# Attention and mixture-of-experts layer in float32: the two heads' outputs scaled ahead of one 128-row output projection, VectorE's order at the end of the last pair, and a rearranged beginning

## The reference, cut to what matters

```
t     = tokens * rsqrt(mean(tokens^2) + eps) * rms_w
gates = sigmoid(t @ w_gates)                          # one number per token and head
q, k, v = t @ wq[h], t @ wk[h], t @ wv[h]
attn  = softmax(causal(q @ k.T * scale))
out   = (attn @ v) * gates
pred  = sum over heads of out[h] @ wo[h]
x     = layernorm(tokens + pred)
```

## Time and profile before

| | us |
|---|---|
| median of 3 runs | 685.77 |
| lowest and highest | 682.54 and 686.07 |
| the profiled execution, its own time | 684.56 |
| its span (first to last instruction) | 682.8 |

### The profile page before, as it was taken

How to read it: one execution, slowest core, us unless ns; L and a number is a source line. 1 busy time by engine, 2 the same in 40 slices (tenths; PEclk the granted TensorE clock), 3 DMA queues, 4 the chain that set the end, 5 groups by cost and what they waited for, 6 DMA issues and landing times.

```text
span 682.8 us, 15047 instructions
## 1 busy us (share of the span) xinstructions
PE 632.5 (93%) x5338; PEld 513.3 (75%) x5338; DVE 476.1 (70%) x1556; ACT 407.7 (60%) x881; POOL 124.5 (18%) x245
## 2 busy tenths in 40 slices
PE   5999999999999999999999999999984959898975
PEld 2788888778888877888887788888852628888862
DVE  4987777788777778887677888767782525666634
ACT  5866556686655668766566876655651213665643
POOL 6100000020000000000000000000136531776650
PEclk9999999999999999999999999999997989999998
DMA  6499961179980117995011200000194102222215
GB/s 146 114 160 165 168 89 33 33 134 167 169 123 2 32 32 64 4 5 3 1 33 32 62 2 1 2 1 2 49 328 61 36 27 48 75 76 71 75 53 167
DMA packets 112922, 48.58 MB, mean 71 GB/s; under 512 B 53712, under 2 KB 106192, under 8 KB 112848
## 3 DMA queue, kind: packets, MB, share of 16 engines
q1 hardware_dynamic: 109456, 42.20, 42.4%
q0 software_dynamic: 2560, 5.28, 2.3%
q10 hardware_dynamic: 832, 0.14, 0.1%
HBM read 14.78 MB, written 24.43 MB: 57 GB/s over the span
## 4 chain that ended last, share of the span: by engine, by line
PE 83%; DVE 6%; another core or an unknown queue 3%; issue 3%; ACT 2%; DMA 2%; DVEq 0%; SPq 0%; POOL 0%; POOLq 0%; ACTq 0%
PE ps_o L1297 19%; PE ps_t L1162 19%; PE ps_s L1263 12%; PE ps_s L1265 9%; PE ps_s L1430 6%; PE ps_s L1173 4%; PE ps_o L1307 4%; PE ps_o L1418 3%; PE ps_s L1340 2%; PE ps_s L1170 2%; PE ps_t L1354 2%; DMA act_s<-y_rows 1%; DVE w_now L1113 1%; DVE act_s L1031 1%
## 5 line engine op out<-in xcount | busy, mean ns | idle before, releaser
L1162 PE MATMUL ps_t<-ident,probs 128*128 128x128 f32 x1104 | 174.4, 275 | 12.1 <-POOL probs L473 8.1
L1162 PEld LDWEIGHTS ps_t<-ident,probs 128*128 128x128 f32 x1104 | 136.0, 141 | 52.8 <-issue 17.8
L661 ACT ACTIVATE probs<-probs,nmax 128x128 f32<-128x128 f32 (+15 forms) x128 | 153.5, 1200 | 20.2 <-DVE nmax L969 12.4
L978 DVE COPY probsT<-ps_t 128x512 f32<-128x512 f32 (+3 forms) x160 | 91.2, 570 | 88.8 <-PE ps_t L1162 87.6
L672 ACT ACTIVATE probsT<-ps_t 128x512 f32<-128x512 f32 (+3 forms) x160 | 89.7, 561 | 93.2 <-PE ps_t L1162 91.7
L1263 PE MATMUL ps_s<-k_h,q_hl 128*128 128x512 f32 (+3 forms) x320 | 142.4, 448 | 0.4 <-DVE q_hl L805 0.4
L1297 PE MATMUL ps_o<-probsT,v_sb 128*64 128x128 f32 x2176 | 139.8, 277 | 0.0
L964 DVE TENSOR_SCALAR_CACHE_REDUCE probs<-ps_s 128x512 f32<-128x512 f32 x192 | 128.4, 686 | 1.0 <-PE ps_t L1162 0.3
L1297 PEld LDWEIGHTS ps_o<-probsT,v_sb 128*64 128x64 f32 x2176 | 116.9, 137 | 14.5 <-issue 12.8
L1265 PE MATMUL ps_s<-k_l,q_hl 128*128 128x512 f32 (+3 forms) x320 | 117.1, 366 | 0.0
L538 POOL TENSOR_TENSOR rden<-rsum,gate 128x2 f32<-128x2 f32 x64 | 12.5, 195 | 416.0 <-ACT probs L661 400.8
(11 more groups left out here) (167 smaller groups left out, 751.0 us busy)
## 6 DMA issues: line engine op xcount, KB each, us to landing
x_sorted<-zeros SPq DMA_DIRECT2D x68, 258.0 KB, 9.5
k_h<-k_h SPq DMA_DIRECT2D x32, 128.0 KB, 2.3
k_l<-k_l SPq DMA_DIRECT2D x32, 128.0 KB, 2.3
w_all<-in_L_ffn_W SPq DMA_DIRECT2D x2, 2048.0 KB
xg<-x_sorted SPq DMA_DIRECT2D x48, 65.0 KB
act_s<-y_rows SPq DMA_DIRECT2D x3, 512.0 KB, 6.5
x_acc<-in_L_attn_tokens SPq DMA_DIRECT2D x4, 256.0 KB, 4.4
y_rows<-y_sb,row_all POOLq DMA_INDIRECT x48
```

What stands on the lines that cost most here:

```text
L661: nc.scalar.activation(probs[s % 2][h][:, 0:w], probs[s % 2][h][:, 0:w], ACT.Exp, bias=nmax[:, row], scale=-1.0, accum_out=rsum[:, row]).t ...
L978: nc.vector.tensor_copy(probsT[s % 2][h][:, c * BT:c * BT + w // P, :].rearrange("p n i -> p (n i)"), ps_t[1][:, 0:w]).then_inc(moved1, 1)
L1162: return nc.tensor.transpose(dst, src, ident[:, :])
```

## The change

The two heads' outputs are scaled before the projection, so that one projection of all 128 rows gives the sum of both heads. GpSimd now inverts the row sums (a power of -1) and multiplies them by the gate, which VectorE has inverted once in the beginning, writing the factor 64 times side by side for each head into `rden_b`, 128 rows by 128. TensorE transposes that into a free part of `ps_o` right behind the products with v. ScalarE copies the 128 rows of the product into one tile `outT[b]`, VectorE multiplies this by the transposed factors (a new stage, `scale`), TensorE does one product with `wo_p`, and VectorE adds it to `x_acc` in one instruction. In VectorE's list for the end of the last pair the copy `t14b` stands ahead of the first `norm`. In the beginning the first three loads of `x_acc` are issued ahead of the semaphores, ScalarE scales three tiles of every four and GpSimd one, the weights' loads stand ahead of that of `rms_w`, and TensorE does six products of `mask` with itself, 128 by 256, whose results are not used.

```
--- before.py
+++ after.py
...
     LAST = len(PIECES) - 1
+    WARM = 6
...
@@ -102,6 +103,8 @@
                 stages.append([("turn", s - 1, h, c, w) for h in range(2) for c, w in chunks[s - 1]])
             if 2 <= s < NT + 2:
                 stages.append([("times_v", s - 2, 0, c, w) for c, w in pv_groups(s - 2)])
+                if scaled:
+                    stages.append([("scale", s - 2, 0, 0, len(pv_groups(s - 2)))])
...
                 for i, x in enumerate(units):
                     place = s + (i + PLACE.get(x[0], 0.5)) / len(units) + lag.get(x[0], 0.0)
+                    if x[0] == "scale" and x[4] == 1:
+                        place -= 0.2
...
-    DVE_UNITS = [pair_units(False, DVE_LAG),
-                 ending(ahead(pair_units(True, DVE_LAG), unit("times_wo", 10), unit("stats", c=n0)),
-                        [wo12, unit("stats", c=n1), unit("norm", c=n0), t14b, pv14, wo13, t15a, t15b, pv15,
-                         unit("norm", c=n1), wo14, unit("stats", c=n2), wo15, unit("stats", c=n3)])]
+    sc13, sc14, sc15 = (unit("scale", s, w=1) for s in range(NT - 3, NT))
+    DVE_UNITS = [pair_units(False, DVE_LAG, True),
+                 ending(ahead(pair_units(True, DVE_LAG, True), unit("times_wo", 10), unit("stats", c=n0)),
+                        [wo12, unit("stats", c=n1), sc13, t14b, unit("norm", c=n0), pv14, wo13, t15a, t15b, pv15,
+                         unit("norm", c=n1), sc14, sc15, wo14, unit("stats", c=n2), wo15, unit("stats", c=n3)])]
...
-        outT = [[sb(f"outT{b}{h}", [P, P], f32, attn) for h in range(2)] for b in range(2)]
+        outT = [sb(f"outT{b}", [P, P], f32, attn) for b in range(2)]
+        rden_b = [sb(f"rden_b{b}", [P, 2, DH], f32, attn) for b in range(2)]
...
         @block.sync
         def _(sp):
-            for s in (wo_done, pv_done, turned, freed, moved0, moved1, out_ready, acc_done):
-                sp.sem_inc(s, ONE)
             for c in range(NC):
+                if c == NC - 1:
+                    for s in (wo_done, pv_done, turned, freed, moved0, moved1, out_ready, acc_done):
+                        sp.sem_inc(s, ONE)
                 sp.dma_start(x_acc[:, c * BT:(c + 1) * BT, :],
                              tokens[0, c * BANK:(c + 1) * BANK, :].rearrange("(n p) d -> p n d", p=P)).then_inc(x_in[c], 16)
...
-            def second_halves(i):
+            def last_tile(i):
 
                 pool.wait_ge(rms_ready, i + 1)
-                for t in range(i * BT + BT // 2, (i + 1) * BT):
-                    ins = nc.gpsimd.tensor_scalar(xn[:, t, :], x_acc[:, t, :], stat[:, 2, t:t + 1], None, ALU.mult)
...
+                t = (i + 1) * BT - 1
+                nc.gpsimd.tensor_scalar(xn[:, t, :], x_acc[:, t, :], stat[:, 2, t:t + 1], None, ALU.mult).then_inc(xn_rest, 1)
...
-            for b in range(2):
-                for h in range(2):
-                    nc.gpsimd.memset(outT[b][h][:, :], 0.0).then_inc(consts, 1)
...
+                if p == 0:
+                    pool.wait_ge(halves_set, 2)
...
                         row_scale(0)
                     pool.wait_ge(exp_done, p * (2 * NT) + (2 * s + 2))
-                    pool.wait_ge(acc_done, p * NT + (ONE + max(s - 3, 0)))
-                    nc.gpsimd.tensor_tensor(rden[:, s % 4, :], rsum[:, 2 * s:2 * s + 2],
-                                            gate1[:, ORDER[s], bass.ds(p * 2, 2)], ALU.mult).then_inc(gated_sum, 1)
+
+                    if p > 0 or s >= 2:
+                        pool.wait_ge(factor_turned, p * NT + (s - 1))
+                    nc.gpsimd.tensor_tensor(rden[:, s % 4, :], rsum[:, 2 * s:2 * s + 2], minus_one[:, :],
+                                            ALU.pow).then_inc(inverted, 1)
+                    pool.wait_ge(inverted, p * NT + (s + 1))
+                    nc.gpsimd.tensor_tensor(rden_b[s % 2][:, :, :],
+                                            gate1[:, ORDER[s], bass.ds(p * 2, 2)].unsqueeze(2).to_broadcast([P, 2, DH]),
+                                            rden[:, s % 4, :].unsqueeze(2).to_broadcast([P, 2, DH]),
+                                            ALU.mult).then_inc(factor_ready, 1)
...
-            act.dma_start(rmsw[:, :], rms_w.rearrange("(p a) -> p a", a=1)).then_inc(gw_in, 16)
             for w, src in ((K, wk), (Q, wq)):
                 act.dma_start(wkq_p[:, w, :].rearrange("d (a e) -> d a e", a=2),
                               src[0:2].rearrange("h d e -> d h e")).then_inc(start_w, 16)
+            act.dma_start(rmsw[:, :], rms_w.rearrange("(p a) -> p a", a=1)).then_inc(gw_in, 16)
...
-                for t in range(i * BT, i * BT + BT // 2):
+                for t in range(i * BT, (i + 1) * BT - 1):
...
                 def unload(s):
-                    act.wait_ge(pv_done, p * NT + (ONE + s + 1))
-
+
+                    act.wait_ge(factor_turned, p * NT + (s + 1))
                     act.wait_ge(wo_done, p * NT + (ONE + max(s - 1, 0)))
-                    for h in range(2):
-                        rows = slice(h * DH, (h + 1) * DH)
-                        nc.scalar.activation(outT[s % 2][h][rows, :], ps_o[s % 2][rows, 0:P], ACT.Copy).then_inc(out_ready, 1)
+                    nc.scalar.activation(outT[s % 2][:, :], ps_o[s % 2][:, 0:P], ACT.Copy).then_inc(unloaded, 1)
...
             dve.wait_ge(ez_ready, 1)
-            nc.vector.tensor_scalar(gate1[:, :, :], gate1[:, :, :], 1.0, None, ALU.add).then_inc(gate_ready, 1)
-            dve.wait_ge(gate_ready, 1)
-            dve.wait_ge(consts, 7)
+            link(nc.vector.tensor_scalar(gate1[:, :, :], gate1[:, :, :], 1.0, None, ALU.add))
+            nc.vector.reciprocal(gate1[:, :, :], gate1[:, :, :]).then_inc(gate_ready, 1)
+            dve.wait_ge(consts, 3)
...
                             ps_t[1][:, 0:w]).then_inc(moved1, 1)
 
-                def row_factor(s):
-                    dve.wait_ge(gated_sum, p * NT + (s + 1))
-                    link_in(nc.vector.reciprocal(rden[:, s % 4, :], rden[:, s % 4, :]))
+                def scale(s):
+
+                    dve.wait_ge(unloaded, p * NT + (s + 1))
+                    nc.vector.tensor_tensor(outT[s % 2][:, :], outT[s % 2][:, :], ps_o[s % 2][:, 2 * P:3 * P],
+                                            ALU.mult).then_inc(out_ready, 1)
 
                 def add(s):
 
                     t = ORDER[s]
                     dve.wait_ge(wo_done, p * NT + (ONE + s + 1))
-                    first_half = nc.vector.scalar_tensor_tensor(
-                        out=x_acc[:, t, :], in0=ps_o[s % 2][:, P:P + D], scalar=rden[:, s % 4, 0:1], in1=x_acc[:, t, :],
-                        op0=ALU.mult, op1=ALU.add)
+                    nc.vector.tensor_tensor(x_acc[:, t, :], ps_o[s % 2][:, P:P + D], x_acc[:, t, :],
+                                            ALU.add).then_inc(acc_done, 1)
                     if p == PAIRS - 1 and s >= 1:
 
                         dve.wait_ge(acc_done, p * NT + (ONE + s))
                         nc.vector.bn_stats(bn[:, ORDER[s - 1], :], x_acc[:, ORDER[s - 1], :]).then_inc(seen, 1)
-                    link_in(first_half)
-                    nc.vector.scalar_tensor_tensor(
-                        out=x_acc[:, t, :], in0=ps_o[s % 2][:, P + D:P + 2 * D], scalar=rden[:, s % 4, 1:2], in1=x_acc[:, t, :],
-                        op0=ALU.mult, op1=ALU.add).then_inc(acc_done, 1)
...
                     mm.then_inc(z_ready, 1)
 
+            pe.wait_ge(pool_step, 2)
+            for _ in range(WARM):
+                nc.tensor.matmul(ps_s[RING - 1][:, 0:2 * P], mask[:, 0:P], mask[:, 0:2 * P], start=True, stop=True)
             pe.wait_ge(ident_set, 1)
...
                     if j == t:
                         mm.then_inc(pv_done, 1)
+                        pe.wait_ge(factor_ready, p * NT + (s + 1))
+                        turn(ps_o[s % 2][:, 2 * P:3 * P],
+                             rden_b[s % 2][:, :, :].rearrange("p h e -> p (h e)")).then_inc(factor_turned, 1)
 
                 def times_wo(s):
-                    pe.wait_ge(out_ready, p * (2 * NT) + (ONE + 2 * s + 2))
+                    pe.wait_ge(out_ready, p * NT + (ONE + s + 1))
                     if s == 0:
                         pe.wait_ge(pair_wo, p + 1)
-                    for h in range(2):
-                        mm = nc.tensor.matmul(ps_o[s % 2][:, P + h * D:P + (h + 1) * D], outT[s % 2][h][:, :], wo_p[:, :],
-                                              start=True, stop=True)
-                    mm.then_inc(wo_done, 1)
+                    nc.tensor.matmul(ps_o[s % 2][:, P:P + D], outT[s % 2][:, :], wo_p[:, :],
+                                     start=True, stop=True).then_inc(wo_done, 1)
 
...
```

42 lines of the change are left out of this document (18 added, 24 removed).

## The result

| | before | after |
|---|---|---|
| median, 10 runs each, us | 685.66 | 678.31 |
| lowest and highest | 682.36 to 689.11 | 675.9 to 681.52 |
| ratio after to before, 95% interval | | 0.9892, 0.987 to 0.9913 |
| profiled execution, its own time | 684.56 | 678.42 |
| its span | 682.8 | 676.7 |

What follows compares the result with a forecast made beforehand. TensorE's own list was taken to bound the pairs. Loop -7.3, start -0.7 and end -0.5 sum to -8.5 us: 684.56 becomes 676.1 profiled, about 677 as median; forecast's own range 672.5 to 680, overall range 671.5 to 682.5.

Steps and rivals of the forecast that it cites:

- The loop, -7.3 forecast: Pairs of heads: TensorE saves 0.12 us a step over 61 steps, -7.3 us, from -4.9 to -9.8.
- a transpose net: TensorE's loop: the new transpose of rden_b adds net 0.10 us a step, between 0.06 and 0.14.
- the wait of the projection for `scale` near a pair's end: At a pair's end the projection, waiting through one engine more, loses 0.2 to 0.3 us a pair.
- the step's turns: Loop: GpSimd's 1.4 us a step is covered because exponentials run one step's turns ahead of the products with v.
- The slip of 0.5 at a pair's first step: Short first step of a pair: TensorE may slip up to 0.5 us, 1 in the four pairs at most.
- VectorE at `scale`, 5 in 100: Loop rival: VectorE stands at scale while ScalarE's copy waits behind an exponential; +8 us in all, 693; 5 in 100.
- The port rule: Loop: GpSimd and VectorE share ports under an exclusive lock; if paid in full, 22 us a pair on VectorE; not summed.
- The beginning, -0.7 forecast: Start: -1.6 us at the first scores plus 0.9 for inverting the gates, -0.7 us, from +0.2 to -2.0.
- -1.6 us at the first scores: Start: k_h about 1 us earlier and VectorE's pause of 0.64 gone; -1.6 us, from -1.0 to -2.2.
- The end of the last pair, -0.5 forecast: Last pair's end: shorter adds against new scales on VectorE's chain, -0.5 us, from 0 to -1.5.
- the shorter `add`s at -1.0: Last pair's end: four adds on VectorE's chain are one instruction shorter, 0.25 us each, -1.0.
- the `scale`s at +0.5: Last pair's end: three scales come in, two of them on VectorE's chain, +0.5 us.

Runs made afterwards that it cites:

- b3_gpsimd_more: Changed kernel with four more 128x128 multiplications on GpSimd in each step, ahead of the one used; 648.61 us, ratio to before 0.9971.
- a6_turn_ahead: Changed kernel with the transpose of rden_b ahead of the step's products with v instead of behind them; 681.17 us, ratio to before 0.9946.
- a1_old_start: Changed kernel with the beginning of before, the gates still inverted by VectorE; 678.37 us, ratio to before 0.9911.
- a3_old_tail: Changed kernel with the first norm ahead of the copy t14b again in VectorE's list; 642.74 us, ratio to before 0.9884.
- e_after_again: The changed kernel itself, unaltered, run again beside three variants on their chip; 678.92 us, ratio to before 0.9897.
- a5_two_products: Changed kernel with the projection done twice, the first time into an unused part of ps_o; 689.23 us, ratio to before 1.0067.
- c1_before_new_start: Kernel before with the new beginning alone and no reciprocal of the gates; 649.25 us, ratio to before 0.998.

## Why the prediction was right

The forecast was 677 and the median is 678.31, inside the forecast's own range of 672.5 to 680. The mechanism of the loop, which is nearly all of the gain, is borne out part by part. That the attention part's sum comes so close, -8.1 against -8.5, is in part luck: the loop gave 0.7 more than forecast, and the start and the end gave 1.1 less. By the steps of the prediction:

**The loop, -7.3 forecast.** The four stretches of pairs give -2.03 - 2.15 - 2.25 - 1.55 = -8.0 us. Each part has its own measurement: a product 0.217 (taken as 0.22), a transpose net 0.06 (taken as 0.10, bounds 0.06 to 0.14, so the lower bound was right: the transpose shows 0.26, which is 0.15 over the bare 0.11, and the score behind it gives back 0.20). The 0.26 lies above the 0.11 to 0.2 that the prediction wanted to see in the profile, although its own sum let the transpose take over 0.15 to 0.20. 16 x (0.06 - 0.22) = -2.5; the wait of the projection for `scale` near a pair's end, allowed at 0.2 to 0.3, is 0.45 a pair, and against it stands 0.35 less of waiting for ScalarE's copy of the probabilities (2.1 us before in two pairs, 1.4 now). That is -2.4, and -2.2 was measured; 0.2 a pair is not accounted for.

**GpSimd.** The power was bounded at 1.05 and is 0.69 for two columns; the multiplication taken as 0.4 is 0.399. With 1.1 us a step in place of 1.4, and the old multiplication of 0.2 gone, GpSimd's load rose by some 15 us a pair, not 22. TensorE never waited for it. The room that I called the step's turns is real in all steps but one of a pair; that one is not far from its edge (b3_gpsimd_more, a6_turn_ahead). The slip of 0.5 at a pair's first step didn't come.

**VectorE at `scale`, 5 in 100.** Over two pairs VectorE waited 3.0 us for ScalarE's copy of `ps_o`, longest 1.0, and TensorE 0.9 for `scale`. The mechanism exists towards a pair's end, where `k_h` of 1.20 us stands ahead of that copy on ScalarE (from 242.88, with VectorE standing 1.02 us until 244.40), and not behind the long exponentials.

**The port rule.** The estimate that could be made of the Trainium skill ("SBUF — State Buffer", section "SBUF: two separate sides") was 22 us of VectorE's time a pair. VectorE's extreme of 512 keeps its duration (0.685 to 0.686) with GpSimd at 6 or 21.6 us of 120 and with 1.6 us a step more, so nothing of it was paid; the rule itself exempts an instruction that reads PSUM, as this one does, and the trace agrees.

**The beginning, -0.7 forecast, -0.2 measured.** The step "-1.6 us at the first scores" was too large, it was -1.17 up to the gates: `k_h` came 0.72 earlier and not 1.0, since ScalarE's last set of tiles starts 1.02 earlier but is one tile, 0.3, longer, and the pause went from 0.64 to 0.18 and not to nothing. Even of this the 0.46 of the pause can't be put down to the change: a1_old_start, with the old beginning, paused for 0.16. Against that run the gates are only 0.75 earlier (27.57 and 26.82), which is about what `k_h` came earlier, 0.78.
**The end of the last pair, -0.5 forecast, +0.07 measured.** The sign of this small term was wrong. The copy's new place gave 1.0 (a3_old_tail), to which the sum had given nothing; so the other two terms, the shorter `add`s at -1.0 and the `scale`s at +0.5, came to +1.1 and not to -0.5. What failed is the path. The prediction priced VectorE's instructions as if VectorE's list alone set the end; in the changed kernel's chain from the last score to the routing there is no `add`, and it goes round through three engines:

```profile
484.20 0.27 PE ps_o L1163
...
484.50 0.29 ACT outT L695
...
484.81 0.15 DVE outT L990
...
485.01 0.69 DVE probsT L983
```

The transpose of the factors, ScalarE's copy and `scale` now stand ahead of the copy `t14b`, and VectorE stands 0.90 us for ScalarE's copy. From the last score to the transposes behind `t14b` it is 4.42 us, before 4.43: in a3_old_tail, without the new order, it is 5.53. So the new path costs 1.1 and the new order gives 1.1 back. Nor could the last two `add`s give much: before, the router's 16 products on TensorE (`logits`) ended at 499.54, 0.31 ahead of VectorE's copy of them, and with shorter `add`s that copy waits for TensorE (0.17 us in the changed kernel). No run took the `add`s or the `scale`s by themselves.

**What was left alone.** The stages behind the pairs took 2.0 us more in the profiled execution. By e_after_again, the same program, it is a difference between executions.

## What to carry to other kernels

Where a group of products makes whoever comes next slower, as the products with v do here, treat that as a price already paid: an instruction put in behind them costs only what it adds beyond it (0.06 us, not its 0.26). Where one engine's list is the bound, a change to it comes through nearly whole (3.0 of 3.5 us a pair in a5_two_products), and a fill of another engine's idle time is free only up to the tightest step; find that step by adding work, not by the mean. In a chain of short waits, as at the start and the end here, take an instruction's cost with its wait, and ask of every earlier arrival which table load or copy it then waits for. And before pricing a small term from one profile, look at the same place in a second execution: the pause of 0.64 that the start was to save was 0.16 in the next.

## What the runs showed of the hardware that was not expected

The same kernel before took 684.24, 685.66 and 686.2 us beside three groups of runs and 650.83 beside the fourth, on another chip. The attention part is the same there (c1_before_new_start: pairs of 120.01 and 120.15, and the routing 0.9 us earlier, as its beginning was 1.0 us shorter); nearly all of the 35 us lies behind it. In the earlier trace rows ScalarE stands for 14.14 us; on that chip the longest wait for the shared expert's activation is 5.7, and the experts' scatters take 69.4 to 69.5 us in place of 82.6 to 86.3. The granted clock from 500 to 530 was 0.83 before and 0.89 after on the other chips (0.77 to 0.92 in all the profiles there), and 1.00 in all four on that one.

What makes TensorE, ScalarE and VectorE stand together on the one kind of chip was not tried here. The ratio of the change doesn't hang on it: 0.9892 and 0.9897 on the one kind, and 0.9896 and 0.9884 for the two nearest variants on the other.

TensorE's clock in the beginning was not the same from execution to execution of one program: the four MATMUL of the first projection took 3.07 in one and 1.88 in the other, behind the same twelve MATMUL of `mask` and a pause of 1.68 and 1.49 us, at a granted clock of 0.50 and 1.00 from 10 to 12 us. Among the variants that keep this beginning they took 1.88 behind a pause of 1.69 in c1_before_new_start, and 3.10 at a granted clock of 0.50 behind one of 1.29 in b3_gpsimd_more, so the length of the pause alone doesn't order them. What does was not tried. The column of the granted clock does not show every slow stretch: before, it has 1.00 from 10 to 12 us, while the same four MATMUL took 3.62.
